# A vision transformer layer on one core: layer norm 1 from PSUM, positions as a two-part product in each block, one residual moved

## The reference, cut to what matters

```
h = einsum('bnf,of->bno', patches, W) + b + pos_emb      # 512 tokens x 256
h = h + attention(layernorm(h))                          # 16 heads of 16, causal, with a slope bias, 16 tokens an image
h = h + ffn(layernorm(h))                                # weights rounded to -1, 0, 1 times a scale; relu squared; a low-rank path

layernorm(x) = (x - mean(x)) / sqrt(var(x) + 1e-5)       # over the 256 features
```

## Time and profile before

| | |
|---|---|
| median of 3 runs | 68.41 us (68.33 to 68.67) |
| profiled execution, whole | 68.16 us |
| its span in the profile | 66.4 us, 2165 instructions |
| TensorE products | 58.6 us busy, 88% of the span |
| TensorE weight loads | 53.1 us, 80% |
| VectorE | 45.3 us, 68% |
| ScalarE | 38.6 us, 58% |
| POOL | 25.9 us, 39% |
| granted TensorE clock | 0.991 of full speed over the span |
| loads | 6.50 MB moved in all, DMA engines busy from 1.7 to about 18 us |

### The profile page before, as it was taken

The page is one execution under the profiler, slowest core; times in us unless marked ns, Lnnn a source line. Parts: engine busy times, 40 slices in busy tenths (PEclk is TensorE's granted clock), DMA queues, the critical chain, the costliest instruction groups (busy, mean ns, idle before and its releaser), DMA issues.

```text
span 66.4 us, 2165 instructions
## 1 busy us (share of the span) xinstructions
PE 58.6 (88%) x894; PEld 53.1 (80%) x894; DVE 45.3 (68%) x97; ACT 38.6 (58%) x78; POOL 25.9 (39%) x43
## 2 busy tenths in 40 slices
PE   5989999999989999999947958999988999999900
PEld 5968588889968999698936846999978999999800
DVE  0000039467999896999799993725999589989660
ACT  5300012824294969974899699830988599783000
POOL 6500007597779569999957100000000000000840
PEclk9999999999999999999999999999999999999996
DMA  0899999999810000000000000000000000000044
GB/s 0 238 352 340 320 392 400 344 387 400 320 42 0 10 0 0 0 10 0 10 0 0 10 5 5 0 10 0 0 0 0 0 0 0 0 0 0 10 161 156
DMA packets 3371, 6.50 MB, mean 98 GB/s; under 512 B 385, under 2 KB 1314, under 8 KB 3362
## 3 DMA queue, kind: packets, MB, share of 16 engines
q1 hardware_dynamic: 3218, 6.24, 26.4%
q10 hardware_dynamic: 144, 0.13, 0.6%
HBM read 5.85 MB, written 0.52 MB: 96 GB/s over the span
## 4 chain that ended last, share of the span: by engine, by line
PE 60%; DVE 18%; ACT 10%; DMA 5%; issue 3%
PE psum L307 12%; PE psum L467 12%; PE psum L493 11%; PE psum L373 5%; PE psum L347 5%; DMA head_sb<-head 5%; PE psum L313 3%; PE psum L402 3%; DVE z L787 3%; PE psum L476 2%; PE psum L327 2%; DVE prob_n L850 2%; DVE bn L779 2%; DVE prob_t L857 2%; ACT zt_hi L610 2%
## 5 line engine op out<-in xcount | busy, mean ns | idle before, releaser
L1051 POOL TENSOR_TENSOR tail_sb<-tail_sb,h 128x256 f32<-128x256 f32 x3 | 2.1, 734 | 25.0 <-DVE tail_sb L886 25.0
L493 PE MATMUL psum<-mlp_t,sq_lo 128*128 128x256 f32 x32 | 7.7, 281 | 0.0
L493 PE MATMUL psum<-mlp_t,sq_hi 128*128 128x256 f32 x32 | 7.7, 280 | 0.0
L601 ACT ACTIVATE std<-mv,eps_sb 128x1 f32<-128x1 f32 x8 | 2.4, 294 | 8.8 <-DVE mv L781 8.8
L777 DVE TENSOR_TENSOR h<-psum,posb 128x256 f32<-128x256 f32 x4 | 1.6, 412 | 8.5 <-PE psum L307 8.5
L467 PE MATMUL psum<-zt_hi,fc_t 128*128 128x256 f32 x32 | 6.9, 287 | 0.5 <-ACT zt_hi L610 0.5
L726 ACT ACTIVATE head_sb<-psum,fc_scale 128x256 f32<-128x256 f32 x16 | 6.7, 471 | 0.7 <-DVE kqv_sb L897 0.7
L467 PE MATMUL psum<-zt_lo,fc_t 128*128 128x256 f32 x32 | 6.7, 279 | 0.0
L493 PEld LDWEIGHTS psum<-mlp_t,sq_lo 128*128 128x128 f32 x32 | 6.0, 189 | 0.0
L493 PEld LDWEIGHTS psum<-mlp_t,sq_hi 128*128 128x128 f32 x32 | 6.0, 189 | 0.0
L307 PE MATMUL psum<-head_sb 128*128 128x256 f32 x24 | 5.7, 389 | 0.3 <-DMA head_sb<-head 0.3
(11 more groups left out here) (112 smaller groups left out, 158.8 us busy)
## 6 DMA issues: line engine op xcount, KB each, us to landing
head_sb<-head SPq DMA_DIRECT2D x6, 256.0 KB, 3.7
fc_sb<-w_fc SPq DMA_DIRECT2D x2, 512.0 KB, 6.9
mlp_sb<-w_mlp SPq DMA_DIRECT2D x2, 512.0 KB, 8.7
tail_sb<-tail SPq DMA_DIRECT2D x2, 384.0 KB, 5.9
out<-tail_sb SPq DMA_DIRECT2D x3, 128.0 KB, 1.7
kqv_sb<-w_k SPq DMA_DIRECT2D x1, 256.0 KB, 6.3
kqv_sb<-w_q SPq DMA_DIRECT2D x1, 256.0 KB, 6.5
kqv_sb<-w_v SPq DMA_DIRECT2D x1, 256.0 KB, 5.8
```

What stands on the lines that cost most here:

```text
L493: mm = pe.matmul(mlp_ps[f * BH + b], part[:, n % RING, a, b * P:(b + 1) * P], mlp_t[:, 2 * j + a, :], start=j == 0 and a == 0 and i == 0 a ...
L601: nc.scalar.activation(std[:, which, b:b + 1], mv[:, which, b, 1:2], ACT.Sqrt, bias=eps_sb[:, 0:1]).then_inc(std_ready, 1)
```

## The change

- The position product moves into each block's own PSUM sum. It is now an fp32r product (`embed_pos`) in two parts: the position rows stand twice in the tile, as rows 0 to 16 and 32 to 48 (rows 17 to 31 are zero), 49 rows in all (`POS_ROWS`). ScalarE rounds the tile to fp32r (`pos_r`); VectorE replaces the values of rows 32 to 48 by what the rounding left off. One product over 49 rows then adds high and low part. The load has 49 rows instead of 17. There are four such products instead of one fp32 product, and `posb` is gone.
- For tiles 4 and 5 TensorE again does blocks 0 and 1 in turn; the position product of a block closes its sum.
- VectorE's add is gone. `bn_stats` and the normalise of layer norm 1 read `tok_ps[b]` in PSUM. h1 is now written by four ScalarE copies (`hidden_copy`), behind z of the block. `value(0)` and `key(1)` get a wait on these copies, since they overwrite the banks.
- In VectorE's list `stats1(2)` goes ahead of `zt_low(0)` and `normalise1(3)` ahead of `key_copy(0)`.
- `ident_bf` and `select_r` are made by ScalarE instead of POOL; the low part of the V weights goes ahead of `bias_parts` on POOL; the residual of half 1 goes from behind half 0's to behind the rounding of the FFN weights and `value_factors`.

```diff
-        pos_sb = sb("pos_sb", [S + 1, P + E])
-        posb = sb("posb", [P, E])
+        pos_sb = sb("pos_sb", [POS_ROWS, P + E])
+        pos_r = sb("pos_r", [POS_ROWS, P + E], F32R)
...
-                return pe.matmul(tok_ps[b], lhs, head_sb[:, k, HT:HT + E], start=k == 0, stop=k == KF - 1)
+                return pe.matmul(tok_ps[b], lhs, head_sb[:, k, HT:HT + E], start=k == 0, stop=False)
+
+            def embed_pos(b, stop=False):
+                return pe.matmul(tok_ps[b], pos_r[:, 0:P], pos_r[:, P:P + E], start=False, stop=stop)
...
-            pe.wait_ge(pos_in, 16)
-            pe.matmul(pos_ps, pos_sb[:, 0:P], pos_sb[:, P:P + E], start=True, stop=True).then_inc(pos_done, 1)
-            for b in range(BH):
-                for k in range(LAST, KF):
-                    pe.wait_ge(head_in[k], 16)
-                    mm = embed(k, b)
-                mm.then_inc(tok_done, 1)
+            for k in range(LAST, KF):
+                pe.wait_ge(head_in[k], 16)
+                for b in range(BH):
+                    embed(k, b)
+                    if k == KF - 1:
+                        pe.wait_ge(pos_step, 2)
+                        embed_pos(b, stop=True).then_inc(tok_done, 1)
...
             turn(1, z, zt_ps[1], z1_ready, zt_turned)
+            pe.wait_ge(h1_ready, 3)
             value(0)
             score_bias(0)
             scores(0)
             pe.wait_ge(k_copied, 1)
+            pe.wait_ge(h1_ready, BLOCKS)
             key(1)
...
-            copy_out(posb[:, :], pos_ps, pos_done, 1, posb_ready)
+            def hidden_copy(b):
+                act.wait_ge(z1_ready, b + 1)
+                nc.scalar.activation(h1[:, b, :], tok_ps[b], ACT.Copy).then_inc(h1_ready, 1)
+
+            act.wait_ge(pos_in, 16)
+            nc.scalar.activation(pos_r[:, :], pos_sb[:, :], ACT.Copy).then_inc(pos_step, 1)
             norm_std(0, 0, var1, std1)
             norm_std(1, 0, var1, std1)
+            act.wait_ge(const_in, 16)
+            nc.scalar.activation(ident_bf[:, :], ident, ACT.Copy).then_inc(ident_half, 1)
             weight_high(K, k_in, k_w_hi)
             weight_high(Q, q_in, q_w_hi)
             copy_out(zt_hi[0][:, :, :], zt_ps[0][:, :], zt_turned, 1, zt_hi_ready)
             norm_std(2, 0, var1, std1)
             weight_high(V, v_in, v_w_hi)
+            nc.scalar.activation(select_r[:, :, :], select.rearrange("p (o s) -> p o s", o=1).broadcast_to(
+                [P, HPG, S]), ACT.Copy).then_inc(select_done, 1)
+            hidden_copy(0)
+            hidden_copy(1)
             norm_std(3, 0, var1, std1)
+            hidden_copy(2)
+            hidden_copy(3)
...
-            dve.wait_ge(posb_ready, 1)
+            low_rows = slice(POS_LOW, POS_ROWS)
+            low_part(pos_r[low_rows, P:P + E], pos_sb[low_rows, P:P + E], pos_r[low_rows, P:P + E], 1, pos_step, pos_step)
...
             weight_low(Q, q_w_hi, q_w_lo)
+            weight_low(V, v_w_hi, v_w_lo)
             bias_parts()
-            weight_low(V, v_w_hi, v_w_lo)
...
             residual(0)
-            residual(1)
             hidden_factors()
...
             value_factors()
+            residual(1)
```

More of the change, by code:

```diff
@@ L41 @@
 FOLD = 4 * 2 * RANK
+POS_LOW = 32
+POS_ROWS = POS_LOW + S + 1
 C_ID = 0
@@ L190, in build_program @@
         q_zero = sem("q_zero")
-        pos_done, posb_ready = sem("pos_done"), sem("posb_ready")
+        pos_step = sem("pos_step")
         select_done = sem("select_done")
@@ L522, in _ @@
             for k in range(KF):
-                mm = embed(k, 3)
-            mm.then_inc(tok_done, 1)
+                embed(k, 3)
+            embed_pos(3, stop=True).then_inc(tok_done, 1)
             key(0)
@@ L773, in scales, with stats @@
                 dve.reciprocal(scale[:, 1, :], scale[:, 0, :]).then_inc(scaled, 1)
-            def stats(b, which, hidden_state, src, other, src_done, h_sem, bn_sem, var_sem):
-                dve.wait_ge(src_done, b + 1)
-                dve.tensor_tensor(hidden_state[:, b, :], src, other, ALU.add).then_inc(h_sem, 1)
-                dve.wait_ge(h_sem, b + 1)
-                dve.bn_stats(bn6[:, which, b, :], hidden_state[:, b, :]).then_inc(bn_sem, 1)
+            def stats(b, which, hidden_state, bn_sem, var_sem):
+                dve.bn_stats(bn6[:, which, b, :], hidden_state).then_inc(bn_sem, 1)
                 dve.wait_ge(bn_sem, b + 1)
@@ L910, in _ @@
             normalise1(1)
+            stats1(2)
             zt_low(0)
-            stats1(2)
             normalise1(2)
             stats1(3)
+            normalise1(3)
             key_copy(0)
-            normalise1(3)
             key_spread(0, (3,))
@@ L971, in bias_tables @@
                 pool.wait_ge(const_in, 16)
-                rel_, neg_, select_ = (t.rearrange("p (o s) -> p o s", o=1).broadcast_to([P, HPG, S])
-                                       for t in (rel, neg, select))
-                pool.tensor_scalar(ident_bf[:, :], ident, 1.0, 1.0, ALU.mult, ALU.mult).then_inc(ident_half, 1)
-                pool.tensor_scalar(select_r[:, :, :], select_, 1.0, 1.0, ALU.mult, ALU.mult).then_inc(select_done, 1)
+                rel_, neg_ = (t.rearrange("p (o s) -> p o s", o=1).broadcast_to([P, HPG, S]) for t in (rel, neg))
                 pool.tensor_tensor(alibi[:, :, :], rel_, slope.rearrange("p (h o) -> p h o", o=1).broadcast_to(
@@ L1101 @@
     consts[:, C_VB:C_END] = b_v.T
+    positions = np.zeros((POS_ROWS, P + E), np.float32)
+    for row in (0, POS_LOW):
+        positions[row:row + S, 0:P] = np.tile(np.eye(S, dtype=np.float32), (1, IPB))
+        positions[row + S, 0:P] = 1.0
+        positions[row:row + S, P:] = a(L0_tok_pos_emb)
+        positions[row + S, P:] = a(L0_tok_b)
     arrays = {
         "head": np.concatenate([x_t[:, :, 0:HT], by_partition(a(L0_tok_W).T)], axis=2),
-        "pos": np.concatenate([np.concatenate([np.tile(np.eye(S, dtype=np.float32), (1, IPB)), np.ones((1, P), np.float32)]),
-                               np.concatenate([a(L0_tok_pos_emb), a(L0_tok_b).reshape(1, E)])], axis=1),
+        "pos": positions,
         "tail": x_t[:, :, HT:TOK].reshape(P, KF, BH, P).transpose(0, 2, 1, 3),
```

21 lines of the change are left out of this document (12 added, 9 removed).

## The result

The changed kernel takes 69.77 us (median of 4 runs, 69.37 to 71.08) against 68.54 for the kernel before on the same chip. The ratio is 1.017 (95% interval 1.009 to 1.025): slower, where 67.75 us was forecast.

A forecast was written before the change was run, and what follows sets the result against it. TensorE was read as the busiest engine, with times at 19.5 us carried to the end. Front -0.31, fourth position product +0.155, wait for z -0.49 gave -0.65 from 68.41: 67.75 us, eight-in-ten range 67.4 to 68.5.

The forecast's parts named there:

- old position product goes: At the front, between head tiles 3 and 4: the fp32 position product of 0.62 us on TensorE disappears.
- four new ones: Four fp32r position products on TensorE at 0.155 us each, three ahead of the first transposes, the fourth behind block 3.
- tile 5's wait, and tiles 4 and 5 in time: At the front: TensorE's 0.16 us wait goes; tile 4 lands at 7.26 and tile 5 at 7.96, both in time.
- wait for z of block 3: At the last two transposes, 19.06 us: TensorE's wait for block 3's normalise goes, -0.49 us.
- dear position products: Rival: position products at 0.31 us each instead of 0.155 cost 0.62 more, 68.4 us, no change; chance 0.10.
- it costs 1.74 - 0.70 = 1.04 us of every landing behind it: Front loads: the 17-row position load, in single file through one DMA engine, delays every later head tile by 1.04 us.
- tile 4 still gates: Rival: the 1.04 us has another cause, tile 4 lands near 7.84 plus 0.1, total 68.4 us; chance 0.12.
- The position rows' rounding: Front, ScalarE and VectorE: low rows ready between 7.5 and 7.9, wanted at 8.85, covered by 0.9 us.
- the waits on the hidden copies: At `value(0)` and `key(1)`: last ScalarE copy near 17.7, `value(0)` stands at 18.85, so nothing is late.
- the key copy behind the normalise: VectorE, block 3: key copy ends near 17.9, not later than 18.05 before; 0.7 us of cover left for the scores.
- the residual's move: POOL, half 1: residual done at 38.0, wanted at 45.40; worth nothing either way.
- Reading PSUM costs VectorE nothing that I can see: Layer norm 1: add with a PSUM operand takes 0.41 us, normalise from SBUF 0.42, so no extra cost.

The follow-up runs named there:

- Kernels 1 to 4: Changed kernel with position products over 128 rows: 0.991 of before; over 64 rows: 69.70 us; 17-row fp32: 70.82 us; blocks 0 and 1 side by side: 69.51 us.
- kernels 5 to 8: Kernel before with a 32-row position load: 1.002; without that load: 1.007; before unchanged, profiled twice: 68.58, 68.94 us; changed kernel unchanged: 70.60 us.
- kernel 13: Changed kernel with 128-row position products and the residual of half 1 back beside that of half 0: 0.9895 and 0.994 of before.
- kernel 11: Changed kernel with 128-row position products, layer norm 1 back on SBUF, no ScalarE copies, VectorE's old order: 0.998 of before.
- kernels 9 and 10: Before with block 3's normalise ahead of the key copy: 1.014; changed kernel with 128-row position products and key copy back ahead of that normalise: 0.998.

## Why the prediction was wrong

**The sum by its own steps**, for the profiled executions, up to `value(0)`:

| step | forecast | measured | from |
|---|---|---|---|
| old position product goes | -0.62 | -0.82 | 0.62, and 0.20 behind it: the 20 half-products take 4.54, and 20 x 0.216 is 4.32; the last 0.02 is all that the wait for tile 5 cost |
| four new ones | +0.62 | +1.97 | 4 x 0.31, and 0.20 + 0.20 + 0.13 + 0.20 on the groups behind |
| tile 5's wait, and tiles 4 and 5 in time | -0.16 | +0.66 | block 2 starts at 10.76; less 0.82 of position products 9.94; in before 12.69 - 2.59 = 10.10. So -0.16 in all, with the -0.82 |
| wait for z of block 3 | -0.49 | -0.49 | from 10.76 to 20.82 is 10.06, in before 9.40; of the 0.66 more, 1.15 are position products |
| sum | -0.65 | +1.32 | 20.82 - 19.50 |

**The step that failed** is the price of the position product, "I take 0.155, half of the 0.31 that the pair of 64-row fp32r products takes", within bounds of 0.12 and 0.31. All four cost 0.49 on average. The lower bound was taken from the spacing of products of one kind, where no change-over falls between them. The pair at 20.97 was no ground for halving: its two products start within 0.01 us of each other in the trace, side by side on 64 rows each, and share what change-over there is. The rows for it were in the earlier trace rows: the only product over fewer than 128 rows in that stretch had 0.33 us idle ahead of it and 0.33 behind it. I took both for waits on loads because the releaser column said so. But tile 4 had landed at 7.84 and its weights started at 8.09, 0.25 us later; that didn't fit a wait on the load and should have raised the question. Kernels 1 to 4 show the cause. The rival "dear position products" had the direction, with 0.31 each too small a price. A smaller misreading stands beside it: "0.16 of it the wait for tile 5" took idle time of the weight load for time lost; the products there were held up by 0.02.

**The second step that failed** is "it costs 1.74 - 0.70 = 1.04 us of every landing behind it". The packets did run one behind the other, and the 49 rows of after did run side by side (16 packets of that size in 0.4 us), as the prediction derived. But tile 4 landed at 7.92. What had been unusual was the early landing of tiles 2 and 3 in one execution; in kernels 5 to 8 tile 4 lands between 7.2 and 7.8, with 17, 32, 49 rows ahead of it and with none. No run shows the 1.04. The rival "tile 4 still gates" was the right one here, and the old position product had stood in the shadow of that landing, so that taking it away gave next to nothing. Not in every execution: in the second profile of before it ran from 8.03 to 8.66, behind the landing of tile 4 at 7.78, and there it was in the open.

The prediction priced its rivals only one at a time, and two came together. By its own figures tile 4 adds 0.65 to the forecast and dear products 0.62, which makes 69.0; the 4 x (0.49 - 0.31) = 0.72 that the products cost beyond even that makes 69.7. Measured from 68.41 the ratio of 1.017 is 69.6.

**Behind the front.** Landings and clock move the start of block 2 between 9.94 and 12.02 us, whatever the kernel. From there to the end of the span the profiles agree within 0.1: 56.4 us in three of before, 56.9 and 56.8 in two of after, 56.0 in both of kernel 13, 56.3 in kernel 11, 56.6 in kernels 9 and 10. The loss of after is 0.5 there, and 0.7 ahead of it: in the first profiles it is 2.8 us from the landing of tile 4 to block 2, in before 2.1.

**What held.** The wait for z went, to the hundredth. Its cause was half guessed: 0.42 of the 0.5 us was a normalise from SBUF that took twice as long beside POOL's key spread. The position rows' rounding was in time, the waits on the hidden copies cost nothing, the key copy behind the normalise did no harm, and the residual's move is nothing either way (kernel 13). "Reading PSUM costs VectorE nothing that I can see" is false for the normalise: 0.55 against 0.42, hidden since z was there at 19.15 and wanted at 20.3. In return it isn't slowed: z of block 2 of after took 0.54 under a POOL subtraction of 512 columns that covered it whole (15.86 to 17.13). I had compared it with an add, which takes 0.41 with an operand in PSUM. The Trainium skill (VectorE: DVE Perf Modes, "Why PSUM operands drop a tier") says that an fp32 operation with a PSUM operand loses its faster mode; this row agrees. The range, too, was narrower than one execution's scatter allows: before itself gave 68.16, 68.58 and 68.94 us under the profiler.

**The version to keep** is the change with position products over 128 rows: 0.991 of before, faster than both kernels (with the residual in its old place 0.9895 and 0.994). That is -0.6 us; the sum of the prediction with 0.12 for each product would be -0.65 - 4 x 0.035 = -0.79. Of it 0.27 stands between the start of block 2 and `value(0)`, where 9.13 us (19.25 - 10.12) take the place of 9.40, and 0.4 between block 2 and the end. The rest lies ahead of block 2, where no single profile can tell it from landings and clock.

**Left open:** why before without the position load is slower; what share of the 0.9% layer norm from PSUM has by itself (0.991 and 0.998, with intervals that overlap, and 56.3 against 56.0 behind the front, but kernel 11 differs in list order too and from kernel 13 in the residual); what sets the moment at the front from which TensorE runs at full clock; why 32 warming products cost so much.

## What to carry to other kernels

Before a small product is put among full ones, look in the trace for the nearest product with fewer rows and read the idle time of the weight load on both sides of it; here padding its operands with zeros to 128 rows was the whole difference between a loss and a gain, and where padding can't be had, put such products side by side. A releaser in brackets is an inference: hold it against the landing time. Take nothing on loads or on the first microseconds of TensorE from one execution; measure from a point behind them. Price rivals together as well as apart. And when a wait is removed, find the chain that ends just behind it first.

## What the runs showed of the hardware

- A product over 17, 49 or 64 rows between products over 128 rows costs 0.39 us beyond its own time, in fp32 and in fp32r: 0.51 for an fp32r product of 256 columns that costs 0.12 over 128 rows, 0.82 for an fp32 one, 0.63 for two fp32r ones side by side. Of it 0.33 us shows as idle weight load ahead of the product.
- A normalise of 256 columns on VectorE from SBUF to SBUF takes 0.42 us alone, 0.84 beside POOL's key spread that starts with it (two instructions of 512 columns, 0.7 each), and 0.51 beside two of POOL's bias parts; from PSUM it took 0.54 to 0.55, beside POOL or not.
- `bn_stats` of 256 columns takes 0.43 us from PSUM and from SBUF.
- Half-products start 0.427 us apart at the front and 0.216 apart once the trace has its first entry of full clock, which came at 3.44 to 7.75 us in 20 profiles, at 4.89 and 7.73 in two of one program. The profile's clock view shows that stretch as full.
